# Six attention blocks in one kernel: heads stacked on every fourth row, products by eight heads, shifts made in two steps

## The reference

```python
scores = einsum('bhqd,bhkd->bhqk', q, k)      # masks where there are any
attn   = softmax(scores / sqrt(16), axis=-1)
out    = einsum('bhqk,bhkd->bhqd', attn, v)   # then projection, residual, normalisation, feed-forward
```

## Time and profile before

| | |
|---|---|
| median of 3 runs | 3028.54 us (3007.97 to 3031.79) |
| profiled execution | 2994.87 us |
| its span | 2993.1 us |
| granted TensorE clock, mean | 0.962 of full speed |
| busy: PE, DVE, ACT, POOL | 2741.8, 1894.8, 1559.3, 757.4 us |
| weight loads (PEld, beside PE) | 1969.4 us |
| transfers by SP's queue | 170.8 MB, 35.9% of the 16 DMA engines' span |

### The profile page before, as it was taken

How to read it: one execution, slowest core, us unless ns; L and a number is a source line. 1 busy time by engine, 2 the same in 40 slices (tenths; PEclk the granted TensorE clock), 3 DMA queues, 4 the chain that set the end, 5 groups by cost and what they waited for, 6 DMA issues and landing times.

```text
span 2993.1 us, 57648 instructions
## 1 busy us (share of the span) xinstructions
PE 2741.8 (92%) x22720; PEld 1969.4 (66%) x22720; DVE 1894.8 (63%) x3789; ACT 1559.3 (52%) x2129; POOL 757.4 (25%) x838
## 2 busy tenths in 40 slices
PE   7999998999999999888888888888788899999999
PEld 5666665567777777666565555556555567777777
DVE  5666665555555555767667888887565676555542
ACT  1333333555555554545455565556555666666663
POOL 0011111233333322322223444443122222111111
PEclk9999999899999999989899999989888999999999
DMA  2210102443333343544544544434644553453330
GB/s 91 79 40 26 32 23 34 59 75 51 51 51 59 50 56 45 78 51 67 70 67 67 85 66 66 65 54 68 100 55 56 73 76 54 73 69 59 61 52 15
DMA packets 145968, 177.28 MB, mean 59 GB/s; under 512 B 59404, under 2 KB 66204, under 8 KB 145693
## 3 DMA queue, kind: packets, MB, share of 16 engines
q1 hardware_dynamic: 99622, 170.82, 35.9%
q0 software_dynamic: 46080, 2.79, 1.9%
HBM read 39.67 MB, written 4.19 MB: 15 GB/s over the span
## 4 chain that ended last, share of the span: by engine, by line
PE 73%; DVE 12%; DMA 7%; issue 3%; ACT 3%; SPq 1%; POOL 1%; ACTq 0%; DVEq 0%
PE ps_pv L694 10%; PE ps_nat L521 9%; PE ps_misc L753 9%; PE ps_misc L623 8%; PE ps_st L542 7%; PE ps_misc L775 7%; DMA q_st<-negm_lo 6%; PE ps_misc L649 4%; PE ps_misc L726 4%; DVE mx L1022 4%; PE ps_misc L705 3%; PE ps_nat L525 2%; PE ps_st L546 2%; PE ps_misc L743 2%; ACT pt L858 2%
## 5 line engine op out<-in xcount | busy, mean ns | idle before, releaser
L858 ACT ACTIVATE pt<-ps_st 128x1024 f32<-128x1024 f32 (+1 forms) x768 | 758.0, 987 | 680.9 <-PE ps_st L546 326.9
L1022 DVE TENSOR_REDUCE mx<-ps_nat 128x4 f32<-128x1024 f32 x640 | 780.2, 1219 | 472.7 <-PE ps_nat L521 344.5
L542 PE MATMUL ps_st<-q_st,k_st 51*128 51x256 f32 (+1 forms) x2560 | 333.9, 340 | 124.3 <-DMA q_st<-negm_lo 81.0
L694 PE MATMUL ps_pv<-pt,vaug 128*32 128x256 f32 (+1 forms) x6144 | 423.7, 396 | 0.0
L542 PEld LDWEIGHTS ps_st<-q_st,k_st 51*128 51x128 f32 x2560 | 199.8, 193 | 303.2 <-issue 148.9
L521 PE MATMUL ps_nat<-k_st,q_st 49*128 49x256 f32 (+1 forms) x2560 | 283.5, 299 | 54.1 <-DVE mx L1022 29.6
L1157 POOL TENSOR_TENSOR rstd<-var,half_pow 128x2 f32<-128x2 f32 x144 | 103.0, 716 | 832.3 <-DVE var L909 832.2
L1132 POOL DMA_DIRECT2D q_st<-negm_hi x160 | 97.6, 610 | 815.9 <-DVE negm_lo L1033 815.9
L753 PE MATMUL ps_misc<-xF,weights 128*128 128x256 f32 x1152 | 282.9, 389 | 2.0 <-ACT xF L872 1.4
L521 PEld LDWEIGHTS ps_nat<-k_st,q_st 49*128 49x128 f32 x2560 | 209.4, 197 | 81.6 <-DVE mx L1022 25.3
L694 PEld LDWEIGHTS ps_pv<-pt,vaug 128*32 128x32 f32 x6144 | 166.4, 113 | 131.2 <-issue 33.1
(11 more groups left out here) (118 smaller groups left out, 4232.6 us busy)
## 6 DMA issues: line engine op xcount, KB each, us to landing
qk<-upper SPq DMA_DIRECT2D x640, 128.0 KB, 4.7
qk<-lower SPq DMA_DIRECT2D x320, 128.0 KB, 5.2
weights<-in_weights SPq DMA_DIRECT2D x19, 512.0 KB, 5.9
cT<-in_ctx_t SPq DMA_DIRECT2D x32, 256.0 KB, 3.9
cn<-in_ctx SPq DMA_DIRECT2D x32, 256.0 KB, 2.8
xT<-in_x_t SPq DMA_DIRECT2D x16, 256.0 KB, 3.3
xn<-in_x SPq DMA_DIRECT2D x16, 256.0 KB, 2.8
out<-xn SPq DMA_DIRECT2D x16, 256.0 KB, 3.1
```

The costliest lines, as they stand in the source:

```text
L542: return nc.tensor.matmul(ps_st[:, j, kh, 0:S - q0], lhs, rhs, start=kh == first, stop=last)
L694: last = nc.tensor.matmul(ps_pv[32 * j:32 * j + 32, i % 2, q0:S], vaug[:, rot, kh, s, :], pt[:, at_p, s % 2, kh * S:(kh + 1) * S - q0], st ...
L858: nc.scalar.activation(pt[:, g % PT_SLOTS, :, 0:used], ps_st[:].rearrange("p j a b -> p j (a b)")[:, :, 0:used], ACT.Exp, scale=SCALE).the ...
L1022: last = nc.vector.reduce_max(out, ps_nat[:], AX)
```

## The change

The stack of a head is spread over its group of 64 partitions with a step of 4: features d of part 0, 1 or 2 stand in rows 4d + part, and every fourth row (3, 7, 11, ...) is an extra row. The penalty is row 3, the shift rows are 7 and 11, the others are zero, written once from HBM. So q and k need three transfers each, of 256 KB, from all 128 partitions onto 32 rows, and both score products contract over all 64 rows. Products are computed for eight heads in one step, after four pairs, and pt gets a fifth slot. DVE makes negm_hi straight from PSUM; POOL issues its transfer at once and, after a second wait, that of maxm_lo = max + negm_hi, whose row has -1 on the key side. The operand of `e0` is made in a step of its own, `q0b`, some 0.7 to 1 pair before it. Masks and the penalty row share space with other buffers. The tables of due times have new values in all stages (shown for the first steps of attentions 2 to 4).

```diff
@@ -21,9 +21,10 @@
 SLOT = 2 * HD
 PEN, SHIFT = HD, HD + 1
 GROUP = 64
-PEN_R, SHIFT_R = 3 * HD, 3 * HD + 1
+STEP = 4
+PEN_R, HI_R, LO_R = 3, 7, 11
 ROT = 3
-PT_SLOTS = 4
+PT_SLOTS = 5
 MISC = 3
 LAG = 7
 
...
-    2: [("xtr", 0, -15.3), ("pq", 0, -14), ("pql", 0, -13.7), ("qin", 0, -9.3), ("pk", 0, -9.3),
-        ("kin", 0, -9.1), ("pkl", 0, -9), ("pen", 0, -8.6), ("e0", 0, -5.8), ("len", 0, -5.5),
-        ("kcp", 0, -3.1), ("qcp", 0, -2.9), ("qcp", 1, -2), ("kcp", 1, -0.25), ("pvv", 0, -0.2)],
-    3: [("ldn", 0, -21.3), ("xtr", 0, -14.8), ("ctr", 0, -14.3), ("pq", 0, -10.5), ("qin", 0, -10.45),
-        ("pql", 0, -9.7), ("pk", 0, -9.5), ("pkl", 0, -9), ("kin", 0, -8.1), ("pen", 0, -7.2),
-        ("e0", 0, -6.3), ("len", 0, -5.45), ("qcp", 0, -4.6), ("kcp", 0, -4), ("qcp", 1, -1.8),
-        ("kcp", 1, 0.2), ("pvv", 0, 1)],
...
+    2: [("xtr", 0, -15), ("pq", 0, -14), ("pql", 0, -13.7), ("qin", 0, -9.6), ("pk", 0, -9.3),
+        ("kin", 0, -9.1), ("pkl", 0, -9), ("pen", 0, -8.6), ("q0b", 0, -6.8), ("e0", 0, -5.8),
+        ("qcp", 0, -5.75), ("len", 0, -5.5), ("kcp", 0, -2.5), ("qcp", 1, -2.1), ("kcp", 1, 0.45),
+        ("pvv", 0, 0.5)],
+    3: [("ldn", 0, -20.3), ("xtr", 0, -14.8), ("ctr", 0, -14.3), ("pq", 0, -10.5), ("qin", 0, -9.95),
+        ("pql", 0, -9.7), ("kin", 0, -9.4), ("pk", 0, -9.15), ("pkl", 0, -8.8), ("pen", 0, -7.2),
+        ("q0b", 0, -7), ("e0", 0, -6.3), ("len", 0, -5.75), ("qcp", 0, -4.1), ("kcp", 0, -3.3),
+        ("qcp", 1, -1.7), ("kcp", 1, 1.1), ("pvv", 0, 1.5)],
     4: [("xtr", 0, -12.4), ("pq", 0, -11.2), ("pql", 0, -9.8), ("qin", 0, -9.6), ("pk", 0, -9.4),
-        ("pkl", 0, -9), ("kin", 0, -7.65), ("qcp", 0, -6.8), ("kcp", 0, -3.6), ("qcp", 1, -1.6),
-        ("kcp", 1, 0.75), ("pvv", 0, 2)],
-    5: [("ldn", 0, -24.2), ("clnA", 0, -17.8), ("clnB", 0, -16.9), ("ctr", 0, -14.5), ("xtr", 0, -12.5),
-        ("pq", 0, -10), ("pql", 0, -9.7), ("pk", 0, -9.2), ("pkl", 0, -8.6), ("kin", 0, -6.4),
-        ("kcp", 0, -2), ("qin", 0, -1.85), ("qcp", 0, -1.5), ("pvv", 0, 0), ("kcp", 1, 1.4),
-        ("qcp", 1, 2.7)],
+        ("pkl", 0, -9), ("kin", 0, -7.35), ("qcp", 0, -6.1), ("kcp", 0, -2.6), ("qcp", 1, -1.6),
+        ("kcp", 1, 0.75), ("pvv", 0, 2.5)],
...
-    2: [("otr", 0, 13.85), ("otr", 1, 16.15), ("res", 0, 16.55), ("lnA", 0, 19.2), ("lnB", 0, 21.8),
-        ("msk", 0, 25.3)],
...
+    2: [("otr", 0, 13.05), ("res", 0, 16.05), ("otr", 1, 16.15), ("lnA", 0, 19.2), ("lnB", 0, 22.55),
+        ("msk", 0, 28.4)],
...
@@ -148,8 +149,7 @@
         for i in range(2):
             add(8 * n + 4 * i + 4.6, "nmt", n, i)
             add(8 * n + 4 * i + LAG + 4.4, "pvout", n, i)
-        for c in range(QUADS):
-            add(8 * n + 2 * c + LAG + 2, "pvg", n, c, 2)
+            add(8 * n + 4 * i + LAG + 4, "pvg", n, i, 2)
     return out
 
 
...
-        negm_lo = sb("negm_lo", [16, 2, P])
+        maxm_lo = sb("maxm_lo", [16, 2, P])
...
+        mask0 = on[:, 0, :].bitcast(BF16).rearrange("p (f s) -> p f s", f=2)
+        mask0_t = on[:, 1, :].bitcast(BF16).rearrange("p (f s) -> p f s", f=2)
+        pen_row = xF[0:B, 0, :]
...
 
-            return 16 * 6 * nth((kind, n, 0), lambda m, j: m % 2 == n % 2)
...
                         if i == 0:
-                            sp.dma_start(raw_q[PEN_R:P:GROUP], t["ones"]).then_inc(rows_in, 16)
-                        else:
-                            for row in (SHIFT_R, SHIFT_R + 1):
-                                sp.dma_start(raw_k[row:P:GROUP], t["ones"]).then_inc(rows_in, 16)
-                            sp.dma_start(raw_k[PEN_R:P:GROUP], t["zeros"]).then_inc(rows_in, 16)
+                            sp.dma_start(raw_q[STEP - 1:P:STEP], t["rows"][0]).then_inc(rows_in, 16)
+                        else:
...
@@ -438,9 +436,7 @@
                         else:
                             sp.wait_ge(k_stacked, nth(("kcp", n - 1, 1)))
                         for part, src in enumerate(parts):
-                            for j in range(2):
-                                sp.dma_start(dst[GROUP * j + HD * part:GROUP * j + HD * part + HD],
-                                             src[64 * j:64 * j + 64]).then_inc(done, 16)
+                            sp.dma_start(dst[part:P:STEP], src).then_inc(done, 16)
                     elif kind == "pen" and a == 4:
...
                     else:
-                        lhs = q_st[GROUP * j:GROUP * j + PEN_R + 1, n % 2, p, hf * P:(hf + 1) * P]
-                        rhs = k_st[GROUP * j:GROUP * j + PEN_R + 1, n % 2, p, 0:keys]
+                        lhs = q_st[GROUP * j:GROUP * j + GROUP, n % 2, p, hf * P:(hf + 1) * P]
+                        rhs = k_st[GROUP * j:GROUP * j + GROUP, n % 2, p, 0:keys]
...
                     elif kind == "e0":
 
-                        pe.wait_ge(q0_ready, nth(e))
+                        pe.wait_ge(q0_ready, nth(("q0b", n, 0)))
...
@@ -676,24 +672,24 @@
                         filled(e, nc.tensor.transpose(bank[0:16, 0:P], mx[:, i, :], ident[:]))
                     elif kind == "pvg":
 
-                        pe.wait_ge(exp_done, nth(("st", n, 2 * i + 1)))
+                        pe.wait_ge(exp_done, nth(("st", n, 4 * i + 3)))
                         if i == 0:
                             if a == 0:
                                 wait_out(pe, ("pvt", n, 0))
                                 wait_out(pe, ("pvt", n, 1))
                             else:
                                 wait_out(pe, ("pvv", n, 0))
-                        if i % 2 == 0:
-                            if count := nth(("pvout", n, i // 2)) - 1:
-                                pe.wait_ge(ote_ready, count)
-                        for kh in range(2):
-                            q0 = kh * P if a == 2 else 0
-                            for j in range(4):
-                                s = 4 * i + j
-                                at_p = (n * PAIRS + s // 2) % PT_SLOTS
-                                last = nc.tensor.matmul(ps_pv[32 * j:32 * j + 32, i % 2, q0:S], vaug[:, rot, kh, s, :],
-                                                        pt[:, at_p, s % 2, kh * S:(kh + 1) * S - q0],
-                                                        start=kh == 0, stop=kh == 1)
+                        if count := nth(("pvout", n, i)) - 1:
+                            pe.wait_ge(ote_ready, count)
+                        for c in range(2):
+                            for kh in range(2):
+                                q0 = kh * P if a == 2 else 0
+                                for j in range(4):
+                                    s = 8 * i + 4 * c + j
+                                    at_p = (n * PAIRS + s // 2) % PT_SLOTS
+                                    last = nc.tensor.matmul(ps_pv[32 * j:32 * j + 32, c, q0:S], vaug[:, rot, kh, s, :],
+                                                            pt[:, at_p, s % 2, kh * S:(kh + 1) * S - q0],
+                                                            start=kh == 0, stop=kh == 1)
                         last.then_inc(pv_done, 1)
                     elif kind == "otr":
...
                             m, p = divmod(g - PT_SLOTS, PAIRS)
-                            act.wait_ge(pv_done, nth(("pvg", m, p // 2)))
+                            act.wait_ge(pv_done, nth(("pvg", m, p // 4)))
                         used = 3 * P if a == 2 else 2 * S
                         nc.scalar.activation(pt[:, g % PT_SLOTS, :, 0:used], ps_st[:].rearrange("p j a b -> p j (a b)")[:, :, 0:used],
                                              ACT.Exp, scale=SCALE).then_inc(exp_done, 1)
                     elif kind == "pvout":
-                        act.wait_ge(pv_done, nth(("pvg", n, 2 * i + 1)))
+                        act.wait_ge(pv_done, nth(("pvg", n, i)))
 
                         wait_filled(act, ("otr", n - 1, i))
...
                         out_of_bank(e, last)
-                    elif kind == "e0":
+                    elif kind == "q0b":
                         wait_out(dve, ("pq", n, 0))
...
@@ -1026,12 +1022,14 @@
 
                         if n > 0:
                             dve.wait_ge(*shifted(n - 1, i))
-                        out_of_bank(e, nc.vector.tensor_scalar(negm_t[:, i, :], bank[0:16, 0:P], FLOOR, -1.0, ALU.max, ALU.mult))
-                        if a > 0:
-                            wait_out(dve, e)
-                            link(nc.vector.tensor_copy(negm_hi[:, i, :], negm_t[:, i, :]))
-                            nc.vector.tensor_tensor(negm_lo[:, i, :], negm_t[:, i, :], negm_hi[:, i, :].bitcast(F32),
-                                                    ALU.subtract).then_inc(negm_split, 1)
+                        if a == 0:
+                            out_of_bank(e, nc.vector.tensor_scalar(negm_t[:, i, :], bank[0:16, 0:P], FLOOR, -1.0, ALU.max, ALU.mult))
+                        else:
+                            nc.vector.tensor_scalar(negm_hi[:, i, :], bank[0:16, 0:P], FLOOR, -1.0,
```

(47 more changed lines are left out.)

39 lines of the change are left out of this document (16 added, 23 removed).

## The result

The kernel after takes 2821.70 us (median of 4, 2818.84 to 2825.91) against 3026.44 for before in the same comparison (4 runs, 3007.97 to 3031.79). The ratio is 0.9335 with a 95% interval of 0.9293 to 0.9376: 204.7 us less.

What follows compares the result with a forecast made beforehand. PE was taken as the bound throughout, with its non-work time in stages 2 to 4. Terms of -75 -15 -22 -25 -50 +22 summed to -165 us, giving a median of 2862 us, range 2790 to 2960.

Steps and rivals of the forecast that it cites:

- The likeliest case: Whole kernel: the forecast itself, faster stack transfers ending most shift waits, spanning 2800 to 2915 us, chance 0.57.
- the q_st copy: PE's weight loads waiting for the stack copy: most of 19.7 us would go, 15 us saved.
- the clock: PE in stages 2 to 4: less time at the lower clock level, 50 us saved, bounds 10 and 74.
- q0b: PE's 28.9 us of q0blk waits: making the operand earlier saves 22 us, bounds 0 and 28.9.
- the shift in two steps: DVE and POOL: second issue 0.57 us earlier, counted inside the 75 us; 17 us if the cover were gone.
- The signs: Checks: bursts over 200 GB/s, negm_lo landings under 4 us, its waits under 10, stage 4 clock above 0.96, among others.
- The term of less cover: Gaps between pairs with little PE work, stages 2 and 4: 14 us lost, plus 8 for DVE in stage 3.
- Stack transfers: DMA stack copies onto spread rows: 258 GB/s instead of 130, taking 75 of 81.0 us off PE's shift waits.
- transfers no faster: Rival: the stack burst stays at 12 us per unit, only 78 us saved, 2950 us; chance 0.15.
- Products by eight: PE: 192 blocks instead of 384, each block less saving 0.09 to 0.18 us, 25 us in all.
- the rival of uncovered gaps: Gaps left by the moved product blocks cost 1.2 us each, making the kernel slower, 3094 us; chance 0.05.
- The median: Step from profiled execution to median of runs: the difference of 33.7 us was carried over unchanged, giving 2863.5, stated as 2862.

Runs made afterwards that it cites:

- the first two runs: Kernel before with only the stack rows spread to every fourth row, 2873.35 us; kernel after with each stack transfer cut in two, 2825.05 us.
- the two runs with the same due times: Kernel after with the due times of before, 2881.27 us; kernel after with those due times and products by four heads, 2823.43 us.

## Why the prediction was right, and where its terms were not

**The direction and the main cause held.** Predicted were -165 us and 2862; measured 2821.7. The likeliest case was the one that came: transfers faster, shift waits gone. Its terms for the spread (75 for the shift, 15 for the q_st copy, 50 for the clock, 140 in all) stand against 150 for the spread alone. The other terms came to 25 us, against 52 measured (6, 44 and 2): q0b had 22 us and is worth 4 to 6, and the shift in two steps had none and is worth 33 to 44. These errors cancel in part, and that is luck. Between profiled executions the same split is 107 us for the spread and 66 for the rest, so the close sum below is in part luck too.

**The signs.** Bursts at 382 GB/s, a shift wait of 2.8 us, q0blk waits of 1.1 us, 5 and 4 us in stages 1 and 5 and stage 4 at 364 us are as foreseen. The longest landing is 4.4 us and not under 4, and the clock of stage 4 is 0.96 and not above it. One sign says that a term is wrong: the waits for maxima and exp were not to pass 100 us together, and they are 38.1 + 66.6 = 104.7 us, against 75.0 before. The term of less cover had 22 us; these two waits alone rose by 29.7.

**Stack transfers: right, and a rate too low.** I took 258 GB/s for the new layout between bounds of 130 and more; it is 382. The estimate from the Trainium skill's port rule (SBUF — State Buffer, "Door 1: The DMA port swizzle": 3.6 us a unit, 436 GB/s) was nearer than the row that I took. The load stretch had a share too small to tell the rate at full share. The rival "transfers no faster" fell with the first two runs. The term itself, 75 of 81.0 us, measured 78.2.

**The q_st copy: wrong.** 15 us were to go; the wait of PE's weight loads is 21.4 us against 19.7. ACT's own wait for the transfers did go, from 53.7 to 2.4 us. But all 11 waits of PE for the copy were in stage 3, and in that stage ACT's copy waited for no transfer even before: it waited 1.9 us, for PE. (With fast transfers and the old due times it is 20.9 us, also all in stage 3.) So the copy comes late in ACT's order there. What holds ACT up no run isolates.

**The shift in two steps: the largest miss.** I counted latency and gave it nothing of its own, with 17 us if the cover were gone. It is 44 us on the old order, 33 on the new. "DVE loses one operation" stood there without a price. That operation had a mean of 421 ns, 67 us over 160 calls, and this stood in the groups by line of the profile before:

```profile
L1032 DVE CAST negm_hi<-negm_t 16x128 fp32r<-16x128 f32 x160 | 67.3, 421 | 5.5
```

I read its 0.22 us off one unit instead. That is the usual case (median 216 ns), but 33 of the 160 casts last 0.52 to 1.29 us, and the trace of before shows what these have in common:

```profile
1219.00 1.28 POOL L1154 TENSOR_TENSOR xn<-xn,on 128x512 f32<-128x512 f32 x1 [6.89 <-DVE on L1054]
...
1219.09 1.27 DVE L1032 CAST negm_hi<-negm_t 16x128 fp32r<-16x128 f32 x1
```

Each of the 33 runs beside a tensor_tensor of POOL and ends 0.07 to 0.09 us after it; none of the other 127 has one beside it, and each takes 0.21 to 0.22 us. Of the 33, 15 are in stage 2, 16 in stage 3 and 2 in stage 4. So the cast cost 21.2 us in stage 2 and 23.8 in stage 3, of an engine at 388 of 454 us there, and only 6.9 in stage 1. These are the stages that got shorter without it. The operations left in its place read PSUM: maxm_lo runs beside such a POOL operation 33 times in the kernel after and always takes 0.28 us.

**q0b: right sum, wrong cause.** 28.9 us of waits fell to 1.1. Placing q0b ahead is worth 4 to 6 us; the waits go with the lighter DVE (15.9 us with the cast put back) and the new due times (23.8 us are left with the old ones, 12.0 with products by four besides).

**Products by eight: the busy time, not the time.** Each block saved takes 0.19 us less (0.09 to 0.18 predicted), 36.5 us in all between the two runs with the same due times. The 0.09 us that I called the entry is not one. From natural scores to products it is 0.43 us in the earlier trace rows, where the natural scores had idle time before them, and 0.44 in the median of such cases, but 0.33 where they had none, as at 2001.89 above; to the other work that follows them it is 0.43 and 0.33 us, nearly the same (medians, kernel before). The price lies in the block itself: 16 matmuls take 1.00 us to the next instruction (median, before) and 32 take 1.86 (median, after), at the full clock, so two blocks cost 0.14 us more than one of twice the size. The bill comes in waits for exp and for the copy, and the net of the part with its due times is 2 us instead of my 25 less 22: close in sum. Alone it made before slower by 27 us, as in the rival of uncovered gaps, at 0.14 us net for each block (27 / 192).

**64 rows** cost nothing that shows: from the transposed scores to the natural ones it is 0.34 us in the median with 64 rows and with 51.

**The clock.** From the stages' PEclk the time at the lower level in stages 2 to 4 is 2 x (0.05 x 416 + 0.04 x 364) = 71 us, 106 less than 177; at 42% that is 45 us, 50 predicted. Stage 3 kept its 0.95; with products by four and the due times of before it has 0.99.

**The median.** The sum against the profiled execution was good to 8 us (165 predicted, 172.7 measured). I carried the difference of 33.7 us between that execution and the median over unchanged. It didn't carry: the kernel after has its profiled execution at 2822.13 and its median at 2821.70. The difference goes with the granted clock. The profiled execution of before had a mean of 0.962; among the 12 runs of before in the first comparison, the ones at 3000.1 and 3003.8 us had 0.961 and the others, at 3018 to 3040 us, 0.942 to 0.951. The runs of after all have 0.979 to 0.981 and lie within 7 us. Of the miss of 40 us, 34 are this step of the sum and 8 its terms, less the 1.5 that I rounded off. What makes the clock vary from run to run isn't shown. Slow transfers alone don't explain it: after with adjacent rows spreads over 15 us, but before with the spread alone over 17.

## What to carry to other kernels

Before counting the bytes or transfers of a copy within SBUF, look at the GB/s against the DMA share in its burst. Here a full share moved 130 GB/s where the loads' rate came to 258, which asked for another placement of the rows, and the small transfers of another queue paid for it. Price every instruction that is taken off the engine that is fullest after the bound one, even where its latency is hidden, and by its sum in each stage: a median hides the few calls that stand beside another engine's long operation. A larger block on PE is only as good as the due times around it: measure it together with them, and the old ones with the old block.

## What the runs showed of the hardware

A stack transfer of 128 KB onto 16 adjacent partitions lands in 4.7 to 5.2 us (medians), the same bytes onto 16 partitions with step 4 in 2.3, and 256 KB onto 32 of them in 2.5 to 2.6. At full DMA share bursts of the first move 130 GB/s, bursts of the last 382. 8 KB from POOL's queue land in 1.7 us at the least, and in up to 10.6 us beside bursts of the first kind, 4.4 beside the last. The Trainium skill (SBUF — State Buffer, "Door 1: The DMA port swizzle") gives 109 and 436 GB/s for 4 and 16 ports; the runs agree in kind, and differ by some 20 and 12%. By that rule each halved transfer reaches 8 ports. The kernel is as fast with them as with 16, but as issuing sets the rate of their bursts, this is no test of 8 ports.

The cast of 16 x 128 on DVE, which reads and writes SBUF, took 214 ns at the least, 216 in the median and 421 on average. In all of its 33 slow cases it ran beside a tensor_tensor of POOL and ended just after it. In the same trace negm_t, which reads PSUM, had one beside it 33 times and took 0.27 us, as alone, and the row maxima, also from PSUM, 205 times and took 1.22 us against 1.23 alone. Two other small operations with operands in SBUF behave as the cast does: rec<-rec,tmask takes 0.18 us alone and 1.20 in the median of its 27 cases beside POOL, q0blk 0.23 alone and 1.32 in its 5 cases beside POOL, of 32. Not all do: a reduction of xn, also in SBUF, takes 0.67 us beside POOL and 0.66 alone. So the step q0b had a part of this too. No run moved a POOL operation away, so the wait is read from the traces and not tried.
